# Experts' attention on one core: the maxima turned by one matmul into 48 partitions, and three of the average's steps moved one step on

## The reference, cut to what matters

```python
def expert_step(acc, params):
    qw, qb_, kw, kb_, vw, vb_, ow, ob_, g = params
    q = (x @ qw.T + qb_).reshape(B, S, H, Dh).transpose(0, 2, 1, 3)      # B 2, S 512, H 16, Dh 8
    k = (x @ kw.T + kb_).reshape(B, S, H, Dh).transpose(0, 2, 1, 3)
    v = (x @ vw.T + vb_).reshape(B, S, H, Dh).transpose(0, 2, 1, 3)
    p = jax.nn.softmax(jnp.einsum('bhqd,bhkd->bhqk', q, k) * scale, axis=-1)
    o = jnp.einsum('bhqk,bhkd->bhqd', p, v)
    o = o.transpose(0, 2, 1, 3).reshape(B, S, E) @ ow.T + ob_
    return (acc + o * g[..., None], None)
out, _ = jax.lax.scan(expert_step, jnp.zeros_like(x), (qW, qb, kW, kb, vW, vb, oW, ob, gates))
```

## Time and profile before

| | |
|---|---|
| median of 3 runs | 2183.87 us (2181.33 to 2192.77) |
| the profiled execution | 2187.13 us, of which the span of the core is 2185.3 us |
| PE busy | 1855.6 us, 85% of the span |
| DVE busy | 1673.8 us, 77% |
| ACT busy | 1288.2 us, 59% |
| POOL busy | 941.1 us, 43% |
| mean granted clock | 0.942 |

### The profile page before, as it was taken

One profiled execution on the slowest core, in us unless ns is written; L12 is line 12 of the kernel. 1 busy time (PEld: TensorE's weight loads), 2 busy tenths in 40 slices (PEclk: granted clock), 3 DMA queues, 4 the chain that ended last, 5 costly groups with the idle time before them and its releaser, 6 DMA issues. The chain is left out here.

```text
span 2185.3 us, 50731 instructions
## 1 busy us (share of the span) xinstructions
PE 1855.6 (85%) x20464; PEld 954.8 (44%) x20464; DVE 1673.8 (77%) x2850; ACT 1288.2 (59%) x1848; POOL 941.1 (43%) x914
## 2 busy tenths in 40 slices
PE   5758999999999999999947898988888988988984
PEld 3542233233233333333223665665665655665663
DVE  3856777777777777777647978889878889879873
ACT  4423666666666666666725656666655656656652
POOL 0011111111111111111029958768768768768760
PEclk8956999999999999999968999999999999999998
DMA  1032223222323232323014333333333333333320
GB/s 36 1 76 50 49 57 58 50 55 55 64 60 65 60 64 60 64 60 61 2 39 119 89 95 103 100 96 107 95 96 103 100 95 103 100 96 102 95 69 15
DMA packets 101281, 156.36 MB, mean 72 GB/s; under 512 B 29335, under 2 KB 64185, under 8 KB 97209
## 3 DMA queue, kind: packets, MB, share of 16 engines
q1 hardware_dynamic: 98937, 152.19, 28.5%
q10 hardware_dynamic: 2112, 0.94, 0.3%
HBM read 98.03 MB, written 51.12 MB: 68 GB/s over the span
## 5 line engine op out<-in xcount | busy, mean ns | idle before, releaser
L824 DVE TENSOR_REDUCE ENM<-PM 128x1 f32<-128x512 f32 x1024 | 665.4, 687 | 212.3 <-PE PM L604 199.9
L735 ACT ACTIVATE EPT<-PA 128x1024 f32<-128x1024 f32 x512 | 514.6, 1021 | 214.7 <-PE PV L627 124.2
L604 PE MATMUL PM<-EKX,EQX 48*128 48x512 bf16 x1024 | 381.3, 393 | 18.9 <-DVE ENM L824 17.9
L1300 POOL TENSOR_TENSOR DRN<-DRN,DHALF 128x8 f32<-128x8 f32 x192 | 371.7, 1936 | 0.0
L524 POOL CAST ENMP<-ENM 128x16 bf16<-128x16 f32 x64 | 12.7, 198 | 748.0 <-DVE ENM L824 748.0
L627 PE MATMUL PV<-EPT,EVP 128*32 128x256 f32 x4096 | 327.9, 392 | 2.1 <-ACT EAVS L766 1.9
L1298 POOL TENSOR_TENSOR DQR<-DR 128x512 f32<-128x512 f32 x192 | 252.5, 1315 | 169.0 <-DVE DR L1581 169.0
L616 PE MATMUL PA<-EQX,EKX 51*128 51x512 bf16 x1024 | 254.6, 387 | 19.4 <-DMA EQX<-EROWS 15.4
L1344 PE MATMUL PM<-DWQKV,DXS 128*128 128x512 f32 x384 | 214.4, 641 | 26.9 <-ACT DRAW L1500 20.3
L604 PEld LDWEIGHTS PM<-EKX,EQX 48*128 48x128 bf16 x1024 | 93.8, 93 | 308.9 <-DVE ENM L824 222.0
L1500 ACT ACTIVATE DRAW<-PM 128x512 f32<-128x512 f32 x192 | 114.6, 597 | 169.5 <-DVE DR L1581 93.1
(11 more groups left out here) (207 smaller groups left out, 2858.2 us busy)
## 6 DMA issues: line engine op xcount, KB each, us to landing
DV<-d_vpark SPq DMA_DIRECT2D x192, 256.0 KB, 4.9
d_vpark<-DVT SPq DMA_DIRECT2D x48, 512.0 KB, 2.6
e_park<-EPARTS SPq DMA_DIRECT2D x64, 192.0 KB, 3.0
EQX<-e_park SPq DMA_DIRECT2D x32, 384.0 KB, 5.6
EKX<-e_park SPq DMA_DIRECT2D x32, 384.0 KB, 9.2
DWQKV<-in_WqkvR SPq DMA_DIRECT2D x6, 1536.0 KB, 10.0
e_park<-EPARTS SPq DMA_DIRECT2D x64, 128.0 KB, 2.7
e_park<-EPARTS SPq DMA_DIRECT2D x64, 64.0 KB, 2.1
```

Of the source, the lines that this page charges most:

```text
L604: pe.matmul(PM[:, r, :], lhsT=QX[64 * r:64 * r + KQ, b, hp, t * 128:(t + 1) * 128], rhs=KX[64 * r:64 * r + KQ, b, hp, :], start=True, stop ...
L735: s_.activation(PT[:, kt, pair * 2 * S:(pair + 1) * 2 * S], PA[:, 2 * pair:2 * pair + 2, :].rearrange("p a b -> p (a b)"), ACT.Exp, scale= ...
L824: v.tensor_reduce(NM[:, g % 2, t, j, 0:1], PM[:, r, :], AX.X, ALU.max, negate=True).then_inc(maxed, 1)
L1300: g.tensor_tensor(rn, rn, HALF[:, 0:8], ALU.pow).then_inc(rooted.sem, 1)
```

## The change

Three things change, all of them in `stage_b`.

- NM is laid out so that the 48 values of a query tile's partition (4 heads, 3 parts, 4 query tiles) are contiguous. One matmul with 48 columns of weights turns them into 48 partitions of 128 queries, where four matmuls of 12 columns turned them into 12 partitions of 512.
- ROWS is 48 partitions by 128. ACT's copy is 48x128 in place of 12x512. The four DMAs remain; each now takes 12 partitions of 256 bytes to 3 partitions of four pieces of 256 bytes, in place of 3 partitions of 1,024 bytes.
- "v" moves from step 5 to step 6, "ont" from 5 to 6, and "o" from 6 to 7, on PE and ACT through `slot_uses`, and DVE's addition of "o" with them.

```diff
     if g % HG == 1 and more:
-        u += [(5, "v")]
+        u += [(6, "v")]
     if g % HG == 0 and not (first and g == 0):
-        u += [(5, "ont"), (6, "o")]
+        u += [(6, "ont"), (7, "o")]
...
-        NM = m.sb("ENM", [128, 2, TB, 4, 3])
-        NMP = m.sb("ENMP", [128, TB, 4], BF16)
-        ROWS = m.sb("EROWS", [12, 2, S], BF16)
+        NM = m.sb("ENM", [128, 2, 4, 3, TB])
+        NMP = m.sb("ENMP", [128, 4, TB], BF16)
+        ROWS = m.sb("EROWS", [12 * TB, 2, 128], BF16)
...
                 def turn_maxima(e, g, n):
                     pe.wait_ge(max_parted, (e * NG + g) + 1)
-                    turn4(lambda t: NM[:, g % 2, t, :, :].rearrange("p j s -> p (j s)"), n)
+                    scratch(n)
+                    turn(m, pe, PX[0:12 * TB, 0:128], NM[:, g % 2, :, :, :].rearrange("p j s t -> p (j s t)")).then_inc(filled, 1)
...
-                    s_.activation(ROWS[:, g % 2, :], PX[0:12, :], ACT.Copy).then_inc(drained, 1)
+                    s_.activation(ROWS[:, g % 2, :], PX[0:12 * TB, 0:128], ACT.Copy).then_inc(drained, 1)
...
-                        act.dma_start(QX[at:at + 3, g // HG, 2 * (g % HG) + j // 2, :], ROWS[3 * j:3 * j + 3, g % 2, :]).then_inc(rows_in, 16)
+                        act.dma_start(QX[at:at + 3, g // HG, 2 * (g % HG) + j // 2, :].rearrange("s (t q) -> s t q", t=TB),
+                                      ROWS[12 * j:12 * j + 12, g % 2, :]).then_inc(rows_in, 16)
...
-                        if s == 6 and "o" in uses:
+                        if s == 7 and "o" in uses:
                             add_out(gp // HG, use(e, g, "o"))
```

More of the change, by code:

```diff
@@ L523, in split_maxima @@
                     pool.sem_inc(pool_passed, 1)
-                    gp.tensor_copy(NMP[:, :, :], x[:, :, :, 0]).then_inc(max_step, 1)
+                    gp.tensor_copy(NMP[:, :, :], x[:, :, 0, :]).then_inc(max_step, 1)
                     pool.wait_ge(max_step, 3 * k + 1)
-                    gp.tensor_tensor(x[:, :, :, 1], x[:, :, :, 0], NMP[:, :, :], ALU.subtract).then_inc(max_step, 1)
+                    gp.tensor_tensor(x[:, :, 1, :], x[:, :, 0, :], NMP[:, :, :], ALU.subtract).then_inc(max_step, 1)
                     pool.wait_ge(max_step, 3 * k + 2)
                     pool.sem_inc(pool_passed, 1)
-                    gp.tensor_copy(NMP[:, :, :], x[:, :, :, 1]).then_inc(max_step, 1)
+                    gp.tensor_copy(NMP[:, :, :], x[:, :, 1, :]).then_inc(max_step, 1)
                     pool.wait_ge(max_step, 3 * k + 3)
-                    gp.tensor_tensor(x[:, :, :, 2], x[:, :, :, 1], NMP[:, :, :], ALU.subtract).then_inc(max_parted, 1)
+                    gp.tensor_tensor(x[:, :, 2, :], x[:, :, 1, :], NMP[:, :, :], ALU.subtract).then_inc(max_parted, 1)
                 def slot(e, g, first, last):
@@ L823, in maxima @@
                         dve.wait_ge(qscored, (e * NG + g) * 16 + (2 * s + r + 1))
-                        v.tensor_reduce(NM[:, g % 2, t, j, 0:1], PM[:, r, :], AX.X, ALU.max, negate=True).then_inc(maxed, 1)
+                        v.tensor_reduce(NM[:, g % 2, j, 0, t:t + 1], PM[:, r, :], AX.X, ALU.max, negate=True).then_inc(maxed, 1)
                 def inverse(n):
```

## The result

The changed kernel takes 2212.2 us (median of 4 runs, 2209.3 to 2216.4) against 2182.7 (4 runs) before: a ratio of 1.013 [1.011, 1.016], 29.5 us slower. The forecast was 2190, with a range to 2207: the time lies outside the range, and it is slower where "the same" was forecast. The profiled execution took 2210.1 us, 22.9 more than that of before; a second profile of the changed kernel took 2231.2, 15 above the highest of the four, so its figures stand beside the first one's and not in their place.

The account below looks back on a forecast made before the run. No engine full: DVE, ACT and PE coupled by small buffers, SP's chain setting group 2's start. 2187.1 - 9.3 (turn) - 2.2 (ends) + 17.6 (clock) = 2193.2 us profiled, less 3.3: median 2190, range 2170 to 2207.

Parts of the forecast that it names:

- The turn: One transpose for four and a smaller ACT copy: 0.30 us less per group, counting in groups 2 and 3, 9.3 us.
- issues that are dearer: ACT's four row DMAs in their new shape: 690 ns each against 675, +0.06 us per group.
- The moved steps: Groups 0 and 1: both 0.98 us PE idles go, but 2.7 us new idle before group 2; zero gain in 15 of 16 halves.
- SP's chain: SP's twelve DMAs and bring-in of q and k set group 2's start, so gains in groups 0 and 1 count nothing.
- The clock: Longer PE idle before group 2 lowers the clock: 14 halves, 9 in 10, 1.4 us each, 17.6 us lost.
- a rival at 2.5 us: Low clock lasts after the idle before group 2: 2.5 us in each of 14 halves, 2207 us in all; chance 0.12.

Follow-up runs that it names:

- the last two experiments: Changed kernel with early q bring-in, later weight loads and one filler matmul per group 2, moved steps undone: 2169.7 us; with the turn undone too: 2208.1 us.
- best kernel: Changed kernel with q brought in between the parkings, next expert's weight loads behind the bring-in, one filler matmul ahead of each group 2 wait: 2142.7 us, 0.979 of before.

## Why the prediction was wrong

- **The turn** came out at the number, 0.31 us per group (0.30 forecast), with parts that were off and cancelled, which is luck: the exponential of step 4 comes 0.47 us sooner after the turn's start (0.36 forecast), and the next one gives back 0.10 (0.06) to issues that are dearer by 0.054 each (0.015); these are the figures of the one group shown.
- **The moved steps** were right: both waits for EON gone, groups 0 and 1 shorter, all but 0.2 us of it given back before group 2, whose start stayed (31.5 to 31.3). That this hung on SP's chain is shown by the last two experiments: with the chain shortened, the same steps count about 1.5 us per half.
- **The clock: the term that was mis-sized.** That it falls in nearly all halves was right (14 of 15 in both profiles; 9 in 10 of 14 forecast). The price was 1.4 us, read from a low stretch of 3.4 us. A group 2 with no fall takes 12.74 us, so in 14 halves the falls cost (14.84 - 12.74) x 14 = 29 us in the first profile and (15.51 - 12.74) x 14 = 39 in the second, 2.3 and 3.0 for each of the 13 that fell, against 17.6 in the sum. The price was right for most of them: the other 11 falls of the first profile cost 1.4 each, the other 9 of the second 1.8. The rest is a few halves in which the low level lasts and the group takes 17.7 to 19.5 us, at 4.9 to 6.7 each: two in the first profile, four in the second. The prediction had seen 10.2 us at the low level, priced it as a rival at 2.5 us and gave it 0.12, and left it out of the mean. That rival, at 2207 us, was right in kind and still too small. Why one fall lasts 3.4 us and another 20 stays open.
- **A term put at nothing without a reason: PE's instruction list.** Nothing in the sum stood for the stages after the attention. They cost 10 us in the first profile and 19 in the second. That the change leaves them as they are holds for what is computed, not for where the pieces of a fully written-out list begin. The rows for it were in the trace before: waits for "issue" inside bursts of one form, up to 1.7 us.

The two together are the miss. In the profiled pair: 2.6 us gained up to the first exponential (about 0.6 forecast; this stretch scatters by more than that), 15.4 lost in the attention (about 7 forecast: 17.6 less 9.3 and 1.6), 10.1 in the rest (0).

## What to carry to other kernels

Work taken off an engine that afterwards waits for a DMA is no gain, and on PE it can be a loss: price the idle that it makes by what the clock takes afterwards, and give a low stretch a mean price in which the long sightings count, not the commonest one. Shorten the transfer chain first, then the same edit pays. And when a change adds or removes PE instructions, compare the untouched stages too: an idle over 1.5 us named "issue" in the middle of a burst of one form was the instruction fetch in every case here, and its place depends on everything ahead of it.

## What the runs showed of the hardware

- PE can stand for a 16 KB piece of its instructions (256 of them) in a burst of tiny matmuls (121 in 1.42 us) or transposes: 1.6 to 1.9 us where the DMA engines had been at most 0.10 busy, up to 5.4 where they had been 0.80 or more busy with other transfers. It went on 1.3 to 1.7 us after the piece had landed, in 58 stops of 58. A shift by half a piece moved the sum of five layers from 801 to 819 us and back (813 to 801); one by a whole piece brought no stops (805).
- The low level of the clock outlasted 18.1 us of PE work in 20.5 us.
- One filler of 1.1 us ahead of waits of at most 1.4 us (best kernel) went with a level of 1.00 over 850 us.
- A small fp32 matmul (128x128 weights, 8 columns) costs 0.31 to 0.39 us and counts as two matmuls and two weight loads (10.02 us for 32, 25.2 for 64).
- A DMA that takes 12 partitions of 256 bytes to three partitions issues in 729 ns, that from 3 partitions of 1,024 bytes in 675.
